# A gated two-layer transformer kernel on one core: the attention's output projection is moved from the end of a batch's loop into the first steps of the next batch's loop

## The chip, the cores and the metric

The kernel runs on one core of a Trainium2 chip. The metric is the device time of one execution in microseconds. Engine names in the profile are PE (TensorE), DVE (VectorE), ACT (ScalarE), POOL (GpSimd) and SP (SyncE, which issues the DMAs).

## What is computed

Two gated layers over x of 8 batches x 256 tokens x 512 features: attention, a ternary-weight feed-forward network, linear attention, and a mixture of experts. The change touches the first attention alone:

```
q = layernorm(x) @ Wq.T + bq                  # 32 heads of 16
k, v = ctx @ Wk.T + bk, ctx @ Wv.T + bv       # 8 groups of 16, four heads share a group
w = softmax(q k^T / 4, masked)                # 256 x 256 for each head
out = (w v) @ Wo.T + bo                       # 512 -> 512
x = x + tanh(g_xattn[0]) * out
```

Matrices are split into a high and a low 16-bit part, and a product is taken as three matmuls (high by high, high by low, low by high).

## The kernel before

The program has four phases, one after the other; the change is in phase_a (line 298), the first attention. All engines run hand-written programs in order, and semaphores (`ev[...]`) tie them together; nothing is scheduled by a planner, so the order in the code is the order on each engine.

Each batch b of eight is a body of 32 steps (NS) on ACT, POOL and DVE, and of 35 on PE. Step n of batch b is: PE writes a tile of turned scores (`turned_scores`, lines 610 and 612) into one of two PSUM banks; ACT takes the exponential of it twice, as a 16-bit and as a 32-bit tile (lines 809, 810); POOL subtracts the one from the other to get the low part (line 894); PE multiplies both with V (`times_v`, lines 628 and 630), three steps later. Every four steps DVE normalises one group of heads (`normalise`, lines 1004 to 1008) into the tile `on`.

Between these steps stands the preparation of the following batch, nx = b + 1. PE projects queries (`q_of`, 12 matmuls, lines 137 to 139) in steps 1 and 5 and keys and values (`kv_of`) in steps 3 and 7; DVE adds the biases (`bias_q`, line 956, in steps 1 and 5; `bias_kv`, lines 961 to 964, in steps 3 and 7, behind `low_q`, line 969; `low_kv`, lines 976 and 979, in steps 5 and 9). PE turns queries and keys (lines 574 and 583) in steps 9, 11, 12 and 14; the second half of the first turn waits for `dk1`, the event of line 964. From step 15 on PE computes the unturned scores of nx (`scores`, lines 595 and 598) and DVE their maxima (line 992), from which a second turn of the queries follows (`second`, line 574 again): its last part comes after step 34, and ACT copies it (`take_second`, line 756). POOL also takes apart the inputs of batch b + 2; its layer-norm moments are DVE's, line 922, at step 0.

The last thing in a body is the output projection. PE's `output(b)` (line 635) waits until the last group is normalised, makes eight transposes of `on` (line 639) into the banks BS and BS + 1, which `scores` uses later, and for each of two token tiles 12 matmuls with Wo (line 647, recorded as 137 to 139). Between them ACT takes the high part (line 830) and DVE the low part (line 1092); then DVE adds the bias and the gated residual (lines 1096 and 1099). At the start of the next body PE waits for the copies of the second turn:

```
def body(b, par, more):
    nx = b + 1
    wait("c2", b, 4, 4)
```

At the end of batch 3's body DVE also sums 32 partial sums (line 1104), for which PE waits at the start of batch 4 (line 701). Batches 4 to 7 have on ACT and DVE the cutting of the feed-forward weights to signs (lines 782 and 939). The last batch prepares no next one.

Of the kernel before, what the change touches and what calls it, by code (L numbers as in the profile page):

```python
# [19 lines left out]
ALU = mybir.AluOpType  # L20
ACT = mybir.ActivationFunctionType
# [3 lines left out]
B, S, D = 8, 256, 512  # L25
# [272 lines left out]
def phase_a(nc, a, env):  # L298
# [93 lines left out]
    TQ, TK = (9, 12), (11, 14)  # L392
    FIRST = 15
    NORM = LAG + 4

    NPIECE = 32
    ROUND = 12582912.0
# [29 lines left out]
    def bodies(body):  # L427
        for b in range(B):
            body(b, b % 2, b < B - 1)
# [13 lines left out]
    with nc.Block() as block:  # L443
# [89 lines left out]
        def _(pe):  # L533
            pe.sem_inc(ev["AV"], 4)

            def wait(n, b, count=1, per=1):
                pe.wait_ge(ev[n], b * per + count)
# [94 lines left out]
                                                skip_group_check=True)  # L632
                last.then_inc(ev["AV"], 1)

            def output(b):
                wait("ch", b, 2 * G0, 2 * G0)
                for tt in range(2):
                    for k in range(KC):
                        last = nc.tensor.transpose(bank[BS + tt][:, k * P:(k + 1) * P], on[:, tt, k * P:(k + 1) * P],
                                                   ident[:, :])  # L640
                    last.then_inc(ev[f"To{tt}"], 1)
                if b == 0:
                    pe.wait_ge(o_tp, 16 * 2 * KC)
                for tt in range(2):
                    wait(f"lO{tt}", b)
                    for k in range(KC):
                        last = env["three"](bank[BS + tt][:, :], oTh[:, tt, k, :], oTl[:, tt, k, :],
                                            woh[:, k, :], wol[:, k, :], k == 0, k == KC - 1)
                    last.then_inc(ev[f"O{tt}"], 1)


            for t in range(2):
# [41 lines left out]
# [3 lines that stand above are left out]
                wait("lv0", b)  # L697
                wait("lv1", b)
                if b == 4:
                    pe.wait_ge(t_part, 1)  # L700
                    nc.tensor.matmul(bank[BM + 1][:, 0:2], ones[:, :], sums[:, :], start=True,
                                     stop=True).then_inc(t_tot, 1)
                for n in range(NS + LAG):
                    if n < NS:
                        turned_scores(b, par, n)
                    if n >= LAG:
                        times_v(b, par, n - LAG)
                    if not more:
                        continue
                    for tt in range(2):  # L710
                        if n == PQ[tt]:
                            q_of(nx, tt)
                        if n == PK[tt]:
                            if b == 4 and tt == 0:
                                pe.wait_ge(t_red, 1)
                            kv_of(nx, tt)
                        if n == TQ[tt]:
                            wait(f"lq{tt}", nx)
                            turn_q(nx, tt, "tq")
                        if n == TK[tt]:  # L720
                            turn_k(nx, tt)

                    for m in due(n - 1):
                        scores(nx, 1 - par, m)
                    if n == HALF:
                        second(nx, 0)
                if more:
                    second(nx, 1)
                output(b)
            bodies(body)  # L730

        @block.scalar
        def _(act):
# [19 lines left out]
            def take_second(b, par, tt):  # L753
                for h in range(2):
                    wait("t2", b, 2 * tt + h + 1, 4)
                    nc.scalar.activation(qT[:, par, 8 * h:8 * h + 8, tt * P:(tt + 1) * P],
                                         bank16(BM + h).rearrange("p (j q) -> p j q", j=8), ACT.Copy)\
                      .then_inc(ev["c2"], 1)

            def normal(f, t):  # L760

# [41 lines left out]

            def body(b, par, more):
                for n in range(NS):
                    wait("ST", b, n + 1, NS)
                    wait("AV", b, n + 1, NS)
                    wait("L", b, n + 1, NS)
                    nc.scalar.activation(ph[:, n % NP, :], bank[BST + n % 2][:, :], ACT.Exp)  # L809
                    nc.scalar.activation(prob[:, n % 2, :], bank[BST + n % 2][:, :], ACT.Exp).then_inc(ev["E"], 1)  # L810
                    if summed(b, n) is not None:
                        absolute(summed(b, n))
                    if cut_piece(b, n) is not None:
                        sign(cut_piece(b, n))
                    if b + 2 < B and n in (11, 13):
                        normal(b + 2, (n - 11) // 2)
                    if not more:
                        continue
                    for tt in range(2):
                        if n == PQ[tt] + 2:  # L820
                            high_q(b + 1, tt)
                        if n == PK[tt] + 2:
                            high_kv(b + 1, 1 - par, tt)
                    if n == min(HALF + 1, NS - 1):
                        take_second(b + 1, 1 - par, 0)
                if more:
                    take_second(b + 1, 1 - par, 1)
                for tt in range(2):
                    wait(f"To{tt}", b)
                    nc.scalar.activation(oTh[:, tt], bank[BS + tt][:, :].rearrange("p (k c) -> p k c", k=KC), ACT.Copy)\  # L830
                      .then_inc(ev[f"hO{tt}"], 1)
            bodies(body)

        @block.gpsimd
        def _(pool):
# [69 lines left out]
        def _(dve):  # L905
# [105 lines left out]
                    .broadcast_to([P, 2, 4, HD0]), ALU.mult))  # L1011


            klink = Chain(dve, k_ch)
            nc.vector.memset(qs[:, :, :, :], 0.0)
            nc.vector.memset(ks[:, :, :, :, :], 0.0)
# [41 lines left out]
            def body(b, par, more):  # L1058
                link = Chain(dve, ev["ch"], b * PER)
                nx = b + 1  # L1060
                if b == 4:
                    scales()
                for n in range(NS):
                    if n >= NORM and (n - NORM) % 4 == 0:
                        normalise(link, b, (n - NORM) // 4)
                    if b + 2 < B and n == 0:
                        moments(b + 2)
                    if b + 2 < B and n == 3:
                        mean(b + 2)
                    if cut_piece(b, n) is not None:  # L1070
                        magnitude(cut_piece(b, n))
                    if not more:
                        continue
                    for tt in range(2):
                        if n == PQ[tt]:
                            bias_q(nx, tt)
                        if n == PK[tt]:
                            low_q(nx, tt)
                            bias_kv(nx, tt)
                        if n == PK[tt] + 2:  # L1080
                            low_kv(nx, 1 - par, tt)
                    for tt in range(2):
                        if n == TQ[tt]:
                            take(nx, 1 - par, tt, "q")
                        if n == TK[tt]:
                            take(nx, 1 - par, tt, "k")
                    for m in due(n):
                        maxima(nx, m)
                normalise(link, b, G0 - 1)
                for tt in range(2):  # L1090
                    wait(f"hO{tt}", b)
                    nc.vector.tensor_tensor(oTl[:, tt], bank[BS + tt][:, :].rearrange("p (k c) -> p k c", k=KC),
                                            oTh[:, tt], ALU.subtract).then_inc(ev[f"lO{tt}"], 1)
                for tt in range(2):
                    wait(f"O{tt}", b)
                    nc.vector.tensor_tensor(on[:, tt, :], bank[BS + tt][:, :], bo[:, :], ALU.add)\
                      .then_inc(ev[f"x{tt}"], 1)
                    wait(f"x{tt}", b, 3)
                    nc.vector.scalar_tensor_tensor(out=X[:, 2 * b + tt, :], in0=on[:, tt, :], scalar=tg[:, 0:1],
                                                   in1=X[:, 2 * b + tt, :], op0=ALU.mult, op1=ALU.add)  # L1100
                assert link.n == PER, link.n
                if b == 3:
                    dve.wait_ge(t_use, NPIECE)
                    nc.vector.reduce_sum(sums[:, :], part[:, :].rearrange("p (m u) -> p m u", m=2), AX_X).then_inc(t_part, 1)
            bodies(body)
    st.close()


# [1378 lines left out]
```

## Time and profile before

| | |
|---|---|
| median of 3 runs | 1948.77 us (1947.23 to 1953.24) |
| the profiled execution's own time | 1954.19 us |
| its span | 1952.4 us |
| granted TensorE clock, mean over the span | 0.95 |
| PE busy | 1677.2 us (86%) |
| VectorE busy | 1077.9 us (55%) |
| ScalarE busy | 736.4 us (38%) |
| GpSimd busy | 828.0 us (42%) |
| first exponential of batches 0, 1, 2, 7 | 70.19, 139.84, 207.23, 569.91 us |
| last residual of batch 7 starts | 625.34 us |

A row of the timeline has the start in us, the duration in us, the engine, the line, the operation with what it writes and reads, and a count; in brackets stands the idle time of the engine just before it and what ended it. Matmuls overlap, so their spacing, not their duration, is what one costs. The clock is given as a share of 2.4 GHz.

### The profile page before, as it was taken

How to read it: one execution, taken by the hardware profiler on the slowest of the kernel's cores; microseconds unless marked ns; L12 is line 12 of the kernel's file. 1: busy time of each engine (PE TensorE's matmuls, PEld its weight loads, DVE VectorE, ACT ScalarE, POOL GpSimd, SP SyncE). 2: the span in 40 equal slices, each digit the busy share in tenths (PEclk: the TensorE clock that was granted, in tenths of full speed). 3: DMA queues.
4: the chain of work that ended last, by engine and by line, in shares of the span. 5: the costliest groups of instructions: out<-in, count | busy, mean ns of one | idle time of the engine just before them, and what ended most of it. 6: DMA issues, size and time to landing. Idle time of an engine off the chain costs nothing. (4 is left out here: it accounts for less than half of the span.)

```text
span 1952.4 us, 28974 instructions
## 1 busy us (share of the span) xinstructions
PE 1677.2 (86%) x10458; PEld 864.4 (44%) x10458; DVE 1077.9 (55%) x2244; ACT 736.4 (38%) x1326; POOL 828.0 (42%) x853
## 2 busy tenths in 40 slices
PE   5798888887875588888699996999999999888897
PEld 3455545444442243443266563444444444333343
DVE  6678777768663677776155664237755333211126
ACT  2468667666665454444122321221111111122221
POOL 1668656656455344444234532523534342011134
PEclk8999999999987799999799998999999999999999
DMA  5622123123022344443335442734654554366645
GB/s 144 157 66 80 47 55 82 44 55 77 17 68 63 59 97 101 93 93 77 60 69 130 97 87 56 161 88 104 146 112 105 114 124 98 71 151 155 153 132 181
DMA packets 423499, 188.82 MB, mean 97 GB/s; under 512 B 364792, under 2 KB 387576, under 8 KB 423360
## 3 DMA queue, kind: packets, MB, share of 16 engines
q1 hardware_dynamic: 417680, 168.36, 37.9%
q0 software_dynamic: 5680, 18.62, 3.4%
q8 instruction: 86, 1.41, 0.3%
q14 instruction: 53, 0.43, 0.1%
HBM read 77.82 MB, written 22.81 MB: 52 GB/s over the span
## 5 line engine op out<-in xcount | busy, mean ns | idle before, releaser
L894 POOL TENSOR_TENSOR a_pl<-a_prob,a_ph 128x512 f16<-128x512 f32 x256 | 298.5, 1180 | 206.1 <-ACT a_prob L810 204.7
L137 PE MATMUL bank<-XTh,d_whs 128*128 128x512 f16 x512 | 194.7, 380 | 0.9 <-ACT e_y L2256 0.7
L139 PE MATMUL bank<-XTh,d_wls 128*128 128x512 f16 x512 | 194.5, 380 | 0.0
L138 PE MATMUL bank<-XTl,d_whs 128*128 128x512 f16 x512 | 194.5, 380 | 0.0
L809 ACT ACTIVATE a_ph<-bank 128x512 f16<-128x512 f32 x256 | 154.3, 603 | 100.7 <-PE bank L612 77.0
L992 DVE TENSOR_REDUCE a_mx<-bank 128x2 f32<-128x512 f32 x256 | 165.7, 684 | 32.9 <-PE bank L598 29.7
L2094 POOL CAST d_cut<-d_raw 128x512 f16<-128x512 f32 x90 | 58.0, 645 | 234.3 <-DMA d_raw<-in_L_ffn_sw 152.7
L810 ACT ACTIVATE a_prob<-bank 128x512 f32<-128x512 f32 x256 | 155.2, 606 | 0.0
L2014 DVE TENSOR_TENSOR d_hid<-d_hid,bank 128x512 f32<-128x512 f32 x64 | 43.9, 686 | 181.6 <-PE bank L139 179.7
L610 PE MATMUL bank<-a_maddT,ident 128*128 128x512 f16 x256 | 103.4, 404 | 30.1 <-ACT a_prob L810 28.2
L1227 PE MATMUL bank<-b_wfc,b_xTh 128*128 128x512 f16 x256 | 99.5, 389 | 32.3 <-DMA b_xTl<-f_cut 25.9
L1237 PE MATMUL bank<-b_wpj,b_hTh 128*128 128x512 f16 x256 | 104.6, 409 | 22.3 <-DMA b_hTl<-b_hcut 22.3
L2005 ACT ACTIVATE d_hid<-bank 128x512 f32<-128x512 f32 x64 | 38.2, 597 | 213.9 <-PE bank L139 213.9
L2106 POOL DMA_INDIRECT e_x<-rows,d_who x39 | 37.2, 953 | 191.5 <-DMA e_xTl<-e_x 185.2
L595 PE MATMUL bank<-a_madd,ident 128*128 128x512 f16 x256 | 100.0, 391 | 20.5 <-DVE a_mx L992 18.1
L2009 ACT ACTIVATE d_hh<-d_hid 128x512 f16<-128x512 f32 x64 | 40.3, 630 | 191.7 <-DVE d_hid L2014 189.0
L2096 POOL TENSOR_TENSOR d_cut<-d_raw,d_cut 128x512 f16<-128x512 f32 x90 | 105.9, 1177 | 7.2
L2024 DVE SCALAR_TENSOR_TENSOR X<-bank,tg,X 128x512 f32<-128x512 f32 x112 | 76.3, 744 | 50.5 <-PE bank L139 50.5
L1238 PE MATMUL bank<-b_wpj,b_hTl 128*128 128x512 f16 x256 | 103.8, 405 | 0.0
L612 PE MATMUL bank<-a_qT,a_kT 128*128 128x512 f16 x256 | 103.6, 405 | 0.0
L598 PE MATMUL bank<-a_kT,a_qT 128*128 128x256 f16 x512 | 99.7, 277 | 0.0
L1228 PE MATMUL bank<-b_wfc,b_xTl 128*128 128x512 f16 x256 | 99.1, 387 | 0.0
(325 smaller groups left out, 4081.5 us busy)
## 6 DMA issues: line engine op xcount, KB each, us to landing
d_raw<-in_L_ffn_w SPq DMA_DIRECT2D x48, 256.0 KB, 3.0
d_raw<-in_L_ffn_sw SPq DMA_DIRECT2D x42, 256.0 KB, 3.1
made<-e_y SPq DMA_DIRECT2D x39, 256.0 KB
a_stage<-in_L_ffn_w_fc SPq DMA_DIRECT2D x32, 256.0 KB, 2.8
a_stage<-in_L_ffn_w_proj SPq DMA_DIRECT2D x32, 256.0 KB, 3.1
a_fbuf<-in_ctx SPq DMA_DIRECT2D x16, 256.0 KB, 3.7
rows<-f_cut SPq DMA_DIRECT2D x16, 256.0 KB, 2.4
out_x<-X SPq DMA_DIRECT2D x16, 256.0 KB
```

The lines of the kernel that those rows point to most:

```text
L137: nc.tensor.matmul(out_ap, lhi, rhi, start=first, stop=False)
L138: nc.tensor.matmul(out_ap, lhi, rlo, start=False, stop=False)
L139: return nc.tensor.matmul(out_ap, llo, rhi, start=False, stop=last_one)
L610: nc.tensor.matmul(bk[:, :].rearrange("p (r k) -> p r k", r=2), ident16[:, :], maddT[:, kc, :].unsqueeze(1).broadcast_to([P, 2, S]), start ...
L612: nc.tensor.matmul(bk[:, :], kT[:, par, 2 * g + half, kc * P:(kc + 1) * P], qT[:, par, 2 * g:2 * g + 2, :].rearrange("p r q -> p (r q)"), ...
L809: nc.scalar.activation(ph[:, n % NP, :], bank[BST + n % 2][:, :], ACT.Exp)
L810: nc.scalar.activation(prob[:, n % 2, :], bank[BST + n % 2][:, :], ACT.Exp).then_inc(ev["E"], 1)
L894: nc.gpsimd.tensor_tensor(pl[:, n % NP, :], prob[:, n % 2, :], ph[:, n % NP, :], ALU.subtract).then_inc(ev["L"], 1)
L992: nc.vector.tensor_reduce(mx[:, tt, 4 * g + half:4 * g + half + 3:2], bank[BS + m % 2][:, :].rearrange("p (r k) -> p r k", r=2), AX_X, ALU ...
L1237: nc.tensor.matmul(bank[ACC + n % 2][:, :], hTh[:, n % 2, c, :], wpj[:, c, :], start=(c == 0), stop=False)
L1238: last = nc.tensor.matmul(bank[ACC + n % 2][:, :], hTl[:, n % 2, c, :], wpj[:, c, :], start=False, stop=(c == HC - 1))
L2096: nc.gpsimd.tensor_tensor(cut[:, i % RING, 1, :], raw[:, i % RING, :], cut[:, i % RING, 0, :], ALU.subtract).then_inc(p_lo, 1)
```

## The change

The output projection of batch b - 1 is issued inside batch b's loop. PE makes the transposes at step 1 (OTURN), ahead of the query projection of that step, and the 12 matmuls of each token tile at steps 4 and 5 (OUT), in step 5 again ahead of the query projection. ACT takes the high parts at the start of step 2, DVE the low parts at the start of step 2, and the bias and residual at the start of step 6. The last batch's output follows after the loop, as before.

```diff
+    OTURN, OUT = 1, (4, 5)
...
-            def output(b):
+            def turn_output(b):
                 wait("ch", b, 2 * G0, 2 * G0)
                 for tt in range(2):
                     for k in range(KC):
                         last = nc.tensor.transpose(bank[BS + tt][:, k * P:(k + 1) * P], on[:, tt, k * P:(k + 1) * P],
                                                    ident[:, :])
                     last.then_inc(ev[f"To{tt}"], 1)
-                if b == 0:
+
+            def output(b, tt):
+                if b == 0 and tt == 0:
                     pe.wait_ge(o_tp, 16 * 2 * KC)
-                for tt in range(2):
-                    wait(f"lO{tt}", b)
...
+                wait(f"lO{tt}", b)
+                for k in range(KC):
+                    last = env["three"](bank[BS + tt][:, :], oTh[:, tt, k, :], oTl[:, tt, k, :],
+                                        woh[:, k, :], wol[:, k, :], k == 0, k == KC - 1)
+                last.then_inc(ev[f"O{tt}"], 1)
...
                     if n >= LAG:
                         times_v(b, par, n - LAG)
+                    if b and n == OTURN:
+                        turn_output(b - 1)
+                    if b and n in OUT:
+                        output(b - 1, OUT.index(n))
...
-                output(b)
             bodies(body)
+            turn_output(B - 1)
+            for tt in range(2):
+                output(B - 1, tt)
...
                 for n in range(NS):
+                    if b and n == OTURN + 1:
+                        high_output(b - 1)
                     wait("ST", b, n + 1, NS)
...
                 for n in range(NS):
+                    if b and n == OTURN + 1:
+                        low_output(b - 1)
+                    if b and n == OUT[1] + 1:
+                        residual(b - 1)
                     if n >= NORM and (n - NORM) % 4 == 0:
                         normalise(link, b, (n - NORM) // 4)
...
             bodies(body)
+            low_output(B - 1)
+            residual(B - 1)
```

`high_output`, `low_output` and `residual` hold the instructions that stood at the end of the bodies of ACT and DVE, unchanged (lines 828 to 831 and 1090 to 1100); `high_output(B - 1)` follows ACT's loop.

## Rows read from the trace of the kernel before

**Rows 1.** The page, part 1: busy time, share of the span, instructions of each engine.
```profile
PE 1677.2 (86%) x10458; PEld 864.4 (44%) x10458; DVE 1077.9 (55%) x2244; ACT 736.4 (38%) x1326; POOL 828.0 (42%) x853
```
**Rows 2.** Windows: length, busy time of each engine (instructions), granted clock, DMA share, GB/s.
```profile
core 0: us, PE busy (x) PEld busy (x) DVE busy (x) ACT busy (x) POOL busy (x), PEclk, DMA share, GB/s
207.00:217.00 10.00, 10.00 (x82) 5.58 (x81) 7.24 (x15) 7.52 (x16) 7.96 (x8) 1.00 0.00 1
...
570.00:611.00 41.00, 28.96 (x300) 14.79 (x299) 21.51 (x44) 39.87 (x77) 36.05 (x31) 0.79 0.53 116
```
**Rows 3.** Timeline of ACT, seam from batch 1 to 2.
```profile
193.22 0.60 ACT L809 ACTIVATE a_ph<-bank 128x512 f16<-128x512 f32 x1
...
198.13 1.94 ACT L756 ACTIVATE a_qT<-bank 128x1024 f16<-128x1024 f16 x2 [3.82 <-PE bank L574]
199.95 1.09 ACT L830 ACTIVATE a_oTh<-bank 128x512 f16<-128x512 f32 x2
207.23 0.60 ACT L809 ACTIVATE a_ph<-bank 128x512 f16<-128x512 f32 x1 [6.18 <-PE bank L612]
```
**Rows 4.** Timeline of PE, the same seam up to batch 2's step 6.
```profile
197.47 1.07 PE L574 MATMUL bank<-ident,a_qs 128*128 128x128 f16 x16 [1.38 <-DVE a_qs L997]
198.38 1.05 PE L639 MATMUL bank<-ident,a_on 128*128 128x128 f32 x8
201.41 0.39 PE L137 MATMUL bank<-a_woh,a_oTh 128*128 128x512 f16 x1 [1.98 <-DVE a_oTl L1092]
...
206.60 0.38 PE L610 MATMUL bank<-a_maddT,ident 128*128 128x512 f16 x1
...
216.28 0.38 PE L610 MATMUL bank<-a_maddT,ident 128*128 128x512 f16 x1
```
**Rows 5.** Timeline of PE, batch 2's step 9, the second half of the first turn.
```profile
223.14 0.62 PE L574 MATMUL bank<-ident,a_qs 128*128 128x128 f16 x8 [1.75 <-DVE a_k L964]
```
**Rows 6.** Timeline of VectorE, steps 5 to 7 of batch 2.
```profile
218.68 1.28 DVE L979 TENSOR_TENSOR a_v<-a_v 128x128 f16<-128x128 f32 x1
219.93 0.70 DVE L956 SCALAR_TENSOR_TENSOR a_q<-bank,a_bq 128x512 f32<-128x512 f32 x1
...
220.56 0.19 DVE L1004 RECIPROCAL a_rec<-bank 128x8 f32<-128x8 f32 x1
...
222.80 0.28 DVE L964 TENSOR_TENSOR a_k<-bank,a_bkv 128x128 f32<-128x128 f32 x1
```
**Rows 7.** Timeline of VectorE, residual of batch 1's second token tile.
```profile
206.80 0.69 DVE L1096 TENSOR_TENSOR a_on<-bank,a_bo 128x512 f32<-128x512 f32 x1 [1.11 <-PE bank L139]
207.53 0.75 DVE L1099 SCALAR_TENSOR_TENSOR X<-a_on,tg,X 128x512 f32<-128x512 f32 x1
```
**Rows 8.** Timeline of PE and VectorE, first score matmul and later steps, batches 1 and 6.
```profile
139.21 0.38 PE L610 MATMUL bank<-a_maddT,ident 128*128 128x512 f16 x1
...
152.16 0.19 DVE L1004 RECIPROCAL a_rec<-bank 128x8 f32<-128x8 f32 x1
...
156.03 0.27 DVE L964 TENSOR_TENSOR a_k<-bank,a_bkv 128x128 f32<-128x128 f32 x1
...
497.98 0.38 PE L610 MATMUL bank<-a_maddT,ident 128*128 128x512 f16 x1
...
512.53 0.28 DVE L964 TENSOR_TENSOR a_k<-bank,a_bkv 128x128 f32<-128x128 f32 x1
```
**Rows 9.** Instructions of lines 1008 and 1099: ns min/median/max, first and last start.
```profile
L1008 DVE TENSOR_TENSOR a_on<-a_ob,a_rec x64: 291/452/1283, 84.6 to 614.5; 128x128 f32<-128x128 f32 x64
...
L1099 DVE SCALAR_TENSOR_TENSOR X<-a_on,tg,X x16: 750/752/752, 137.6 to 625.3; 128x512 f32<-128x512 f32 x16
```
**Rows 10.** Timeline of PE, seam from batch 3 to 4.
```profile
346.44 0.35 PE L701 MATMUL bank<-a_sums,a_ones 128*128 128x2 f32 x2 [1.76 <-DVE a_sums L1104]
```
**Rows 11.** PE in seams 0 to 1 and 4 to 5; window of seam 5 to 6.
```profile
131.28 1.88 PE L639 MATMUL bank<-ident,a_on 128*128 128x128 f32 x8
...
416.87 0.63 PE L138 MATMUL bank<-a_wol,a_oTh 128*128 128x512 f16 x1
417.30 0.63 PE L139 MATMUL bank<-a_woh,a_oTl 128*128 128x512 f16 x1
...
489.00:498.00 9.00, 7.76 (x28) 3.11 (x28) 2.73 (x4) 1.51 (x3) 0.00 (x0) 0.68 0.00 0
```

## What the change will do: the prediction

> **What bounds the kernel now.** I read the page first [rows 1]: PE is busy for 86% of the span, but that is a mean over stages, and only the first stage, eight batches of attention up to about 626 us, is touched. So I read windows of it [rows 2]. Directly behind the seam between batches 1 and 2, PE is busy for 10.00 of 10.00 us; and in batch 7, which prepares no next batch, ACT is busy for 39.87 of 41 us. The seam itself is seen best from ACT [rows 3]: the last exponential of batch 1 starts at 193.22, then come the copies of the second turn and the two high copies of the output projection, and then ACT idles 6.18 us until the first exponential of batch 2 at 207.23. PE's side [rows 4] shows what fills this: second turn at 197.47, the eight transposes of the output at 198.38, 1.98 us of waiting for VectorE's low part, 24 matmuls from 201.41 to 206.60, and only then the scores of batch 2. There are seven such seams.
>
> The question is what stands next. From the first score matmul of batch 2 (206.60) to that of its step 6 (216.28) [rows 4] PE has no gap: 9.68 us of scores, products with V and the projections of batch 3. Those are the steps into which the output is moved. After them VectorE sets the pace: PE's second group of turned queries waits for VectorE's key bias (line 964) [rows 5], and in program order that stands behind the bias of the second query tile, normalisation 0 and the low query [rows 6].
>
> **The change, part by part.** All times are relative to a batch's first score matmul as it is now ("zero", 206.60 for batch 2), in the seam 1 to 2.
>
> 1. The start. PE need wait only for the copies of the second turn: 198.13 + 1.94 = 200.07 [rows 3]. The batch starts at -6.5 us. That is the gross gain. PE now idles there, from the end of the second turn (198.38, rows 4) for 1.7 us, which the transposes used to fill.
>
> 2. What PE has to issue before step 6: the old 9.68, plus the transposes, 0.93 (their row has 1.05, which holds the tail of the last one; rows 4), plus 24 matmuls, 206.60 - 201.41 = 5.19 [rows 4]. Step 6 is reached at -6.5 + 9.68 + 0.93 + 5.19 = +9.3 instead of +9.7. Of 6.5 us PE keeps 0.4: what goes is the 1.98 us wait, what comes is the 1.7 us wait. No new wait of PE stands in these steps: the high copies (1.09 us on ACT, rows 3) come after step 1, while ACT would wait for step 2's scores behind the query projection anyway; behind them in ACT's queue stands only that exponential. The low parts (VectorE, step 2) stand behind the first query bias and are done about 4 us before PE's step 4.
>
> 3. VectorE. At the seam its four residual operations cover nobody's work; now they stand at step 6, between the second query bias and normalisation 0. One token tile costs 206.80 to 208.28, 1.47 us [rows 7], both 2.9 us. The output matmuls precede the query projection in PE's order, so VectorE doesn't wait for them. Query projection complete at +9.55, bias 0.63 (219.93 to 220.56, rows 6), residual 2.9: normalisation 0 starts at +13.1. Now it starts at 220.56 - 206.60 = +13.96 in batches 2 and 3, and at 152.16 - 139.21 = +12.95 in batches 1, 4 and 5 [rows 6, 8], because VectorE came late from its low key. So the residual takes idle time that the earlier start made.
>
> 4. Contention. Line 1008, with both inputs in SBUF, takes 291 ns at least and 1283 at most [rows 9], the first in the seam, where POOL is idle, the second in the steps. Line 1099 also has both inputs in SBUF and takes 750 to 752 in all 16 cases [rows 9], but all of those stand in a seam. In the steps I bound its extra between 0 and 1.0 us each, the spread of line 1008, and take the middle, 0.5 each: POOL is busy for 7.96 of 10 us in those steps [rows 2], but line 1008 isn't held each time either. Normalisation 0 comes at +14.1. By the Trainium skill, page "SBUF — State Buffer", section "Who interferes with whom", a VectorE instruction with two SBUF inputs and a GpSimd one that reads SBUF exclude each other for a whole instruction; line 1008's spread agrees. By the 750 ns row alone the six batches would be 6 us cheaper than by my sum, by the rule with every instruction blocked 6 us dearer.
>
> 5. From normalisation 0 to the end of the key bias it is 222.80 + 0.28 - 220.56 = 2.5 us in batch 2 and 156.03 + 0.27 - 152.16 = 4.1 in batch 1 [rows 6, 8]. I take 3.3. The key bias ends at +17.4, against +17.1 in batches 1, 4 and 5 and +16.5 in 2 and 3. Everything later in the batch follows it. So +0.3, +0.9, +0.9 us for batches 1 to 3. Batch 6 has no more front work, its key bias ends at 512.53 + 0.28 - 497.98 = +14.8 [rows 8]; the new one is +17.4, less the 1.9 of part 7, hence +0.7.
>
> 6. Seam 3 to 4 holds 1.76 us of PE waiting for a sum that stands behind the residual on VectorE [rows 10]. With the residual moved, the sum is ready while PE waits for the second turn's copies, so 1.8 us go: batch 4 is at +0.3 - 1.8 = -1.5.
>
> 7. Clock. Seam 4 to 5 shows output matmuls at 0.43 us spacing instead of 0.22 (0.63 against 0.38 in duration) [rows 11]; eight of them cost 1.7 us, nine in seam 5 to 6 1.9. The granted clock there was 0.68 of full speed over the seam [rows 11], 1.2 GHz in part of it. If these windows were gone, batch 5 would be at +0.3 - 1.7 = -1.4, batch 6 as given. But PE idles 1.4 us before the second turn [rows 4] and now 1.7 after it, so low-clock windows should come again, in front of a stretch in which every lost PE time counts. I take three of seven at 1.7: +5.1. The bounds are none and seven.
>
> 8. Batch 7. ACT starts 6.5 earlier, does the 1.1 us of copies, and is stopped twice, by PE's 2.6 us (half of 5.19) ahead of steps 5 and 6 each, against an ACT step of 1.3 us on average (41 / 32): about 1.5 each. -6.5 + 1.1 + 3.0 = -2.4. Its own output stays exposed at the end. No queue of SP is passed, since the step issues no DMA, and POOL has none of its work.
>
> Sum: 0.3 + 0.9 + 0.9 - 1.5 - 1.4 + 0.7 - 2.4 = -2.5 us, with the clock **+2.6 us**. The profiled execution took 1954.19 us, of it 1952.4 span; it would take 1956.8. Against the median of the three runs, 1948.77, which is 5.4 lower, the forecast is **1951.4 us**. 0.3% is 5.8 us, about what a measurement of this kernel tells from no change.
>
> **Rivals.**
> *The seam is gone* (3%): 7 x 6.5 = 45 us less, 1903. For it speaks ACT's idle time; against it PE's gapless 9.7 us. PE would need free time in steps 0 to 6, and has none.
> *A part of it stays* (14%): VectorE's operations aren't held (-6), the way to the key bias stays at 2.5 us (-5), and the clock stays up (-5): from there 6 to 13 us less, 1936 to 1943. For it speaks that PE went through seam 1 to 2 at full spacing [rows 4].
> *The residual becomes the wait* (20%). Place: VectorE, step 6. Price: both line-1099 operations held for 1.0 each and 4.1 us to the key bias, 1.8 us over my sum in each of six batches, 11 in all: 1962. It decides from 0.5 us a batch over my sum. For it speaks batch 1 with its 4.1 us; against it batch 2 with 2.5 [rows 6, 8].
> *The clock falls at every seam* (13%): four more windows of 1.7, +7: 1958. The transposes of seam 0 to 1 took 1.88 us for eight against 1.05 [rows 4, 11], so idle time of this size can bring it. The Trainium skill, page "TensorE: Matmul & The Clock Gate", section "HAM oscillation — how this bites in real kernels", says that waits between bursts of matmuls make the clock fall again and again; by that this rival would be the likeliest. The full spacing of seam 1 to 2 is against it [rows 4].
> That the change doesn't do what it says is out: each engine issues in program order.
>
> **How the numbers follow.** Forecast 50%, by itself 1946 to 1954.5. The others as above. Faster by over 0.3%: 3 + 14 = 17%. Slower: 20 + 13 = 33%. Within: 50%. The range reaches down into the partial gain and up to the residual's price: 1941 to 1963.
>
> **What would show it.** Right: in seam 1 to 2 some 7.5 us from the last to the first exponential instead of 14.0; then 15.8 us without a gap on PE up to step 6; ACT idle 3 to 4 us ahead of step 6; PE waiting for line 964 at +17.4. Wrong: gaps on PE in steps 0 to 5, line 1099 at 1.2 us or more with everything behind it late, low-clock matmuls in most seams, or steps 10 to 31 of a batch of another length than now.

## The result, and the profile after

| | before | after |
|---|---|---|
| median | 1951.45 us (20 runs, 1945.20 to 1958.97) | 1957.01 us (20 runs, 1953.27 to 1963.53) |
| ratio | | 1.0025, 95% interval 1.0015 to 1.0035 |
| span of the profiled execution | 1952.4 us | 1951.6 us |
| its first attention stage, first exponential to last residual's start | 70.19 to 625.34 = 555.15 us | 68.61 to 627.73 = 559.12 us |

The change costs a quarter of a per cent: 0.0025 x 1951.45 is 4.9 us more. The forecast was 2.6 more. The spans of the two profiled executions differ the other way, but by less than executions of one kernel differ; the stage alone is 4.0 us longer.

The page of the changed kernel, part 1 (busy time, share, instructions), is to be read beside [rows 1]; the counts are the same:

```profile
PE 1684.2 (86%) x10458; PEld 872.2 (45%) x10458; DVE 1074.7 (55%) x2244; ACT 737.9 (38%) x1326; POOL 831.9 (43%) x853
```

The timeline of ACT in the seam between batches 1 and 2, to be read beside [rows 3]:

```profile
193.56 0.60 ACT L825 ACTIVATE a_ph<-bank 128x512 f16<-128x512 f32 x1
...
198.46 1.94 ACT L764 ACTIVATE a_qT<-bank 128x1024 f16<-128x1024 f16 x2 [3.82 <-PE bank L575]
201.53 0.60 ACT L825 ACTIVATE a_ph<-bank 128x512 f16<-128x512 f32 x1 [1.12 <-PE bank L613]
...
203.45 1.12 ACT L771 ACTIVATE a_oTh<-bank 128x512 f16<-128x512 f32 x2
206.91 0.60 ACT L825 ACTIVATE a_ph<-bank 128x512 f16<-128x512 f32 x1 [2.34 <-PE bank L613]
...
218.31 0.60 ACT L825 ACTIVATE a_ph<-bank 128x512 f16<-128x512 f32 x1 [3.92 <-PE bank L613]
```

The seam has shrunk from 14.0 to 8.0 us, as intended. But ACT now waits 2.34 us for PE ahead of step 2 and 3.92 ahead of step 6. PE's timeline says why, beside [rows 4, 5]:

```profile
197.81 1.07 PE L575 MATMUL bank<-ident,a_qs 128*128 128x128 f16 x16 [1.38 <-DVE a_qs L1010]
200.46 0.61 PE L611 MATMUL bank<-a_maddT,ident 128*128 128x512 f16 x1 [1.58 <-ACT a_qT L764]
200.85 0.63 PE L613 MATMUL bank<-a_qT,a_kT 128*128 128x512 f16 x1
...
203.69 0.38 PE L137 MATMUL bank<-a_wqh,a_xTh 128*128 128x512 f16 x1
...
217.68 0.38 PE L611 MATMUL bank<-a_maddT,ident 128*128 128x512 f16 x1
...
225.25 1.03 PE L575 MATMUL bank<-ident,a_qs 128*128 128x128 f16 x8 [3.12 <-DVE a_k L977]
```

From the first score matmul (200.46) to that of step 6 (217.68) are 17.22 us with no idle time in the trace, where 9.68 stood before. The first matmuls last 0.61 and 0.63 us instead of 0.38. PE then waits 3.12 us for the key bias instead of 1.75. Two windows, the start of the stretch and the whole of it:

```profile
200.40:203.60 3.20, 3.14 (x12) 2.12 (x13) 0.02 (x1) 2.08 (x6) 0.91 (x1) 0.51 0.01 3
200.40:217.70 17.30, 17.24 (x105) 9.46 (x106) 6.47 (x12) 9.01 (x20) 9.42 (x9) 0.91 0.07 17
```

The granted clock is 0.51 of full speed up to the query projection, which is the 1.2 GHz level, and 0.91 over the whole. PE is busy for 17.24 of 17.30 us. VectorE from the second query bias to the key bias, beside [rows 6, 8]:

```profile
217.92 0.71 DVE L969 SCALAR_TENSOR_TENSOR a_q<-bank,a_bq 128x512 f32<-128x512 f32 x1 [2.62 <-issue]
...
218.56 0.67 DVE L1036 TENSOR_TENSOR a_on<-bank,a_bo 128x512 f32<-128x512 f32 x1
219.26 0.75 DVE L1039 SCALAR_TENSOR_TENSOR X<-a_on,tg,X 128x512 f32<-128x512 f32 x1
219.93 0.69 DVE L1036 TENSOR_TENSOR a_on<-bank,a_bo 128x512 f32<-128x512 f32 x1
220.65 0.93 DVE L1039 SCALAR_TENSOR_TENSOR X<-a_on,tg,X 128x512 f32<-128x512 f32 x1
221.51 0.20 DVE L1017 RECIPROCAL a_rec<-bank 128x8 f32<-128x8 f32 x1
...
222.78 0.98 DVE L982 TENSOR_TENSOR a_qs<-a_q,a_qs 128x512 f16<-128x512 f32 x1
...
224.92 0.28 DVE L977 TENSOR_TENSOR a_k<-bank,a_bkv 128x128 f32<-128x128 f32 x1
```

VectorE idles 2.62 us, adds the query bias, and then does the residual (218.56 to 221.51) ahead of normalisation 0, the low query and the key bias, for which PE waits.

Where the 4.0 us of the stage lie, from the two timelines. From the last exponential of the batch before to the end of the key bias, batches 1 to 6: +0.8, +1.8, +2.9, 0.0, +0.2, +2.8, together +8.5. From there to the batch's last exponential: -0.2, -1.9, -2.0, -1.1, -0.3, 0.0, together -5.4. Batch 7 with its seam: -0.6. The rest is in batch 0, whose code is unchanged (+1.3, so not the change's), and behind the last batch (+0.2). Batch 4's 0.0 has in it that the 1.76 us wait of [rows 10] is gone.

### The profile page after: what moved, and what is told of

It reads as the page before. It is cut to its first block and busy times, and to the rows that moved or that the text cites. A ratio compares the mean times of both kernels' runs of the same rounds, so it can differ in the third digit from the quotient of the medians.

```text
span 1951.6 us, 28973 instructions
## 1 busy us (share of the span) xinstructions
PE 1684.2 (86%) x10458; PEld 872.2 (45%) x10458; DVE 1074.7 (55%) x2244; ACT 737.9 (38%) x1326; POOL 831.9 (43%) x853
## 5 line engine op out<-in xcount | busy, mean ns | idle before, releaser
L907 POOL TENSOR_TENSOR a_pl<-a_prob,a_ph 128x512 f16<-128x512 f32 x256 | 304.6, 1203 | 201.3 <-ACT a_prob L826 199.7
L611 PE MATMUL bank<-a_maddT,ident 128*128 128x512 f16 x256 | 107.4, 420 | 37.6 <-ACT a_prob L826 28.0
L1260 PE MATMUL bank<-b_wpj,b_hTh 128*128 128x512 f16 x256 | 107.1, 418 | 23.7 <-DMA b_hTl<-b_hcut 23.7
L596 PE MATMUL bank<-a_madd,ident 128*128 128x512 f16 x256 | 98.8, 386 | 20.7 <-DVE a_mx L1005 18.4
```

Of the source, the lines that this page charges most:

```text
L611: nc.tensor.matmul(bk[:, :].rearrange("p (r k) -> p r k", r=2), ident16[:, :], maddT[:, kc, :].unsqueeze(1).broadcast_to([P, 2, S]), start ...
L907: nc.gpsimd.tensor_tensor(pl[:, n % NP, :], prob[:, n % 2, :], ph[:, n % NP, :], ALU.subtract).then_inc(ev["L"], 1)
L1260: nc.tensor.matmul(bank[ACC + n % 2][:, :], hTh[:, n % 2, c, :], wpj[:, c, :], start=(c == 0), stop=False)
```

## The experiments

The theories. **P**: PE's row of work up to step 6 has no gap, so what the seam gives is paid back there. **V**: the residual at VectorE's step 6 stands ahead of the key bias. **C**: the low clock behind each seam costs on the path. The rival to P is that the moved matmuls are covered and something else eats the seam. In each diff the kernel that it starts from is named.

### One product instead of three, in both kernels

In the changed kernel:

```diff
-                    last = env["three"](bank[BS + tt][:, :], oTh[:, tt, k, :], oTl[:, tt, k, :],
-                                        woh[:, k, :], wol[:, k, :], k == 0, k == KC - 1)
+                    last = nc.tensor.matmul(bank[BS + tt][:, :], oTh[:, tt, k, :], woh[:, k, :],
+                                            start=k == 0, stop=k == KC - 1)
```

> The changed kernel with one product (high by high) instead of three in the output projection: 8 matmuls in a batch instead of 24, 3.5 us of PE time less. The low parts of the output and of Wo are left out of the result. Theory P: step 6 comes 3.5 us earlier; VectorE then waits for its own low key part, so 2.6 us a batch in batches 1 to 6, some 2 in batch 7 and 3.5 at the exposed end: about 21 us less than the changed kernel, ratio to the kernel before 0.992. If PE's work in these steps is covered by others: 3.5 us less, ratio 1.001.

Measured: 0.993 (0.991 to 0.995), that is 18 to 19 us below the changed kernel. The same cut in the kernel before:

> The kernel before with one product instead of three in the output projection (the low parts of the output and of Wo are left out of the result). All of the 24 matmuls stand in a seam there, 3.5 us of them gone in each of eight: 28 us less, ratio 0.986. Under theory P the same cut is worth nearly as much in the changed kernel (19 us were measured from 1.0025 to 0.993), which it could not be if the moved matmuls were covered.

Measured: 0.9867 (0.9837 to 0.9897), 26 us below. There eight cuts of 3.5 us stand bare in the seam and give 26 of 28. In the changed kernel, where seven of them stand beside the loop's work, the runs still gave 18 to 19. Part of that is not the matmuls: in this profile two of the seven seams, those into batches 2 and 4, passed at full clock, and in the changed kernel's none did, which in these two batches is worth 1.5 and 2.2 us (by the two profiles of the next section). Batch 2 shows the rest at full clock: PE's row up to step 6 takes 12.29 us, and 15.75 in the kernel with all three products at full clock (below), so the cut takes 3.5 us out of it. The moved work is not covered, and P holds. But from step 6 to the end of the key bias it now takes 9.79 us instead of 7.51, so of the 3.5 us only about 1.2 reach the key bias. VectorE's timeline in the changed kernel with one product, batch 2:

```profile
212.98 0.28 DVE L992 TENSOR_TENSOR a_v<-a_v 128x128 f16<-128x128 f32 x1
213.22 0.70 DVE L969 SCALAR_TENSOR_TENSOR a_q<-bank,a_bq 128x512 f32<-128x512 f32 x1
```

The second query bias now follows the low parts of key and value without a gap: with less work on PE, VectorE's own chain is the bound, as it was in the kernel before [rows 6].

### Unread matmuls in PE's waits

In the changed kernel, with FILL = (6, 7):

```diff
+            def fill(count):
+                for i in range(count):
+                    nc.tensor.matmul(bank[BST][:, :], woh[:, 0, 0:P], woh[:, 1, :], start=True, stop=True)
...
                 if more:
+                    fill(FILL[0])
                     second(nx, 1)
+                    fill(FILL[1])
```

> The changed kernel with matmuls whose result nobody reads in PE's two waits of the seam: six ahead of the second turn's last part, seven behind it. Theory C (low clock behind the seam costs about 1.5 us in each of seven batches): the first score matmuls of a batch are at 0.22 us spacing again and the eight output transposes at 1.05 us, 7 to 10 us less than the changed kernel, ratio to the kernel before 0.997 to 0.999. If the clock costs nothing on the path: 1.0025, or a little more where the added matmuls are late.

Measured: 0.9972 (0.9959 to 0.9985), 5.3 us below the kernel before and 10.3 below the changed one. PE's timeline of the same seam:

```profile
195.35 1.67 PE L699 MATMUL bank<-a_woh 128*128 128x512 f16 x7
197.09 0.39 PE L612 MATMUL bank<-a_maddT,ident 128*128 128x512 f16 x1
...
198.84 0.38 PE L137 MATMUL bank<-a_wqh,a_xTh 128*128 128x512 f16 x1
```

From the first score matmul to the query projection it takes 1.75 us instead of 203.69 - 200.46 = 3.23: 1.5 us of low clock in this seam. In the changed kernel the first four matmuls of a batch are long (0.59 to 0.63 us) behind all seven seams, in this one (0.38 or 0.39) behind none. PE's row up to step 6 is 15.73 to 15.75 us in batches 1 to 6, and 17.2 to 18.3 in the changed kernel. With the seams, the way from the last exponential to the key bias is shorter by 1.5 to 2.6 us a batch, 12.3 in these six, by the two profiles; batch 7 with its seam is 0.9 longer. C holds, with a price that I had taken for three seams. The Trainium skill, page "TensorE: Matmul & The Clock Gate", section "HAM oscillation — how this bites in real kernels", says that waits between bursts of matmuls bring the clock down each time; its case has longer waits, for DMAs. In the changed kernel the trace agrees, seven of seven, with waits of 1.4 and 1.2 to 1.6 us. Not every such seam is slow: with the same two waits (1.39 and 1.58 us) the kernel with one product went through the seam into batch 2 at full clock.

The kernel before, filled in its own waits (six ahead of the second turn, eight between the output's transposes and matmuls):

```diff
+    FILL = (6, 8)
...
                     last.then_inc(ev[f"To{tt}"], 1)
+                if b < B - 1:
+                    fill(FILL[1])
...
                 if more:
+                    fill(FILL[0])
                     second(nx, 1)
```

> The kernel before with unread matmuls in its own waits of the seam: six ahead of the second turn's last part, eight between the output's transposes and its matmuls. Its low-clock windows in the seams (17 matmuls in two seams, transposes in two more) should go: 4 to 5 us less, ratio 0.9975. Theory P then says that at the same clock the change is worth nothing or little: this run and the changed kernel with the same filling (0.9972) agree within 0.2%. If the seam's 6.5 us had been gained and lost to the clock alone, this one would stay well above the filled changed kernel.

Measured: 0.9989 (0.9972 to 1.0005). All its seams but that into batch 4 are at 14.0 us then, so the two low windows of seams 4 to 5 and 5 to 6 are gone. Between the two filled kernels lie 0.17% or 3.3 us in favour of the change, with overlapping intervals. At the same clock the change is worth about 3 us or nothing, and not 45: P again.

### The residual elsewhere on VectorE

The first of these runs puts it behind the key bias, through a tile of its own, since normalisation 0 overwrites `on` in step 7:

```diff
+    ro = sb("a_ro", [P, 2, D])
...
-                    if b and n == OUT[1] + 1:
+                    if b and n == 8:
                         residual(b - 1)
```

> The changed kernel with the bias and residual of the output at VectorE's step 8 (behind the key bias of step 7) instead of step 6, through a tile of their own. Theory P (PE's gapless row of work from the first score matmul to step 6 pays the seam back): step 6 on PE comes as in the changed kernel. Theory V (the residual on VectorE delays the key bias): normalisation 0 comes 2.9 us earlier, the low query then waits for ACT's high query, which ends 1.3 us before the low query starts now, so the key bias ends 1.3 us earlier in six batches: 6 to 8 us less than the changed kernel, ratio to the kernel before 0.998 to 1.000. If only P holds, the ratio stays at 1.0025.

Measured: 1.009 (1.007 to 1.011): 13 us worse than the changed kernel instead of 6 to 8 better. VectorE's and PE's timelines, batch 2:

```profile
228.16 0.67 DVE L1037 TENSOR_TENSOR a_ro<-bank,a_bo 128x512 f32<-128x512 f32 x1
228.87 1.73 DVE L1040 SCALAR_TENSOR_TENSOR X<-a_ro,tg,X 128x512 f32<-128x512 f32 x1
...
232.09 1.37 DVE L990 TENSOR_TENSOR a_ks<-a_k,a_ks 128x256 f16<-128x256 f32 x1
```
```profile
235.36 0.91 PE L585 MATMUL bank<-ident,a_ks 128*128 128x128 f16 x7 [5.20 <-DVE a_qT L1000]
```

The key bias did come about 1.4 us earlier after the batch's first exponential (22.3 instead of 23.7), as V had it; from PE's step 6 to its end it takes 5.51 us instead of 7.51. But the residual now holds the low key and the copies behind it for 232.09 - 228.16 = 3.9 us, and PE waits 5.20 us for them. V's first half holds, and the assumption that nothing behind the key bias is tight falls.

The second run puts it in step 5, where VectorE idles: the first token tile ahead of the low key, the second between it and the second query bias.

```diff
-            def residual(b):
-                for tt in range(2):
+            def residual(b, tt):
...
-                    if b and n == OUT[1] + 1:
-                        residual(b - 1)
+                    if b and n == OUT[1]:
+                        residual(b - 1, 0)
...
+                        if b and n == OUT[1] and tt:
+                            residual(b - 1, 1)
                         if n == PQ[tt]:
                             bias_q(nx, tt)
```

> The changed kernel with the residual at VectorE's step 5: the first token tile ahead of the low key, the second behind it and ahead of the second query bias, where VectorE waits for ACT and PE (1.5 and 2.6 us in batch 2). Theory V: the low query then waits for ACT's high query instead of the residual, the key bias ends 1.3 us earlier in six batches and nothing behind it is held: 8 us less than the changed kernel, ratio to the kernel before 0.998 to 0.999. Theory P alone (PE sets the key bias): 1.0025, unchanged.

Measured: 0.9993 (0.9977 to 1.0009), 6.2 us below the changed kernel and level with the kernel before. V holds, but the total is near its price of 8 by two errors that offset each other. From PE's step 6 to the end of the key bias it takes 5.50 us instead of 7.51 in batches 1 to 5, and 13.0 us less in six, where I had 8. And "nothing behind it is held" was wrong: from the key bias to the last exponential the six batches are 6.9 us longer than in the changed kernel. VectorE's low part of the values, an operation with both inputs in SBUF, takes 1.23 or 1.24 us instead of 0.28 in five of them, because a subtraction of GpSimd is running when it starts. Residual early and waits filled, both together:

> The residual at step 5 as in the run before and the unread matmuls in PE's two waits of the seam. Theories V and C together, which act on different waits: 8 and 10 us add up, ratio to the kernel before 0.993 (0.991 to 0.995). If they share one path they don't add: 0.997 as with the matmuls alone.

Measured: 0.9918 (0.9894 to 0.9941), median 1936.51 us: the fastest of the kernels here that compute everything. That is 20.9 us below the changed kernel, where the two parts alone had given 6.2 + 10.3 = 16.5; the interval holds that sum too. They act on different waits and add up: PE's row up to step 6 is at 15.73 to 15.75 us, as with the matmuls alone, and from there to the key bias it is 5.50 us, as with the early residual alone. VectorE's timeline of batch 2, and below it GpSimd's row beside the last line:

```profile
212.38 0.68 DVE L1042 TENSOR_TENSOR a_on<-bank,a_bo 128x512 f32<-128x512 f32 x1
213.09 0.75 DVE L1045 SCALAR_TENSOR_TENSOR X<-a_on,tg,X 128x512 f32<-128x512 f32 x1
214.00 1.14 DVE L996 TENSOR_TENSOR a_ks<-a_k,a_ks 128x256 f16<-128x256 f32 x1 [0.16 <-ACT a_ks L766]
...
215.27 0.68 DVE L1042 TENSOR_TENSOR a_on<-bank,a_bo 128x512 f32<-128x512 f32 x1
215.98 0.75 DVE L1045 SCALAR_TENSOR_TENSOR X<-a_on,tg,X 128x512 f32<-128x512 f32 x1
217.50 0.71 DVE L976 SCALAR_TENSOR_TENSOR a_q<-bank,a_bq 128x512 f32<-128x512 f32 x1 [0.77 <-issue]
...
221.09 0.79 DVE L989 TENSOR_TENSOR a_qs<-a_q,a_qs 128x512 f16<-128x512 f32 x1 [1.96 <-ACT a_qs L758]
...
224.78 1.24 DVE L999 TENSOR_TENSOR a_v<-a_v 128x128 f16<-128x128 f32 x1
```
```profile
224.54 1.34 POOL L877 TENSOR_TENSOR a_fcut<-a_fbuf,a_fcut 128x512 f16<-128x512 f32 x1
```

The residual stands in what was idle, and the second query bias is no later for it. What is left ahead of the key bias is 1.96 us of waiting for ACT's high query, and behind it the held low value (224.78). Against the kernel before with its own waits filled (0.9989) the moved output is now worth 0.71% or 14 us, with intervals that stand apart.

### Two more places

The output matmuls in PE's wait for the key bias, with the residual through a tile `ro` as above:

```diff
-    OTURN, OUT = 1, (4, 5)
+    OTURN, OUT = 1, (8, 9)
```

> The changed kernel with the 24 output matmuls in steps 8 and 9 instead of 4 and 5, and the residual at step 10, through a tile of its own; the transposes stay in step 1. Theory P: steps 4 and 5 lose 5.2 us of PE work, step 6 comes 5 us earlier and the key bias 3 to 4; the matmuls fall into PE's wait for the key bias (3.1 us in batch 2), the rest of 2 us and 2.9 us of VectorE come behind it: 1 to 3 us less per batch, ratio to the kernel before 0.990 to 0.998. Theory V alone, or a bound elsewhere: the ratio stays within 0.2% of 1.0025.

Measured: 1.0008 (0.9992 to 1.0024), 3.3 us below the changed kernel with intervals that overlap: less than P had it, and not clearly a gain. The key bias of batch 2 ends 18.4 us after the first exponential instead of 23.7, more than expected; but the residual, then at step 10, stands ahead of the key copies:

```profile
225.78 0.68 DVE L1037 TENSOR_TENSOR a_ro<-bank,a_bo 128x512 f32<-128x512 f32 x1
226.49 1.39 DVE L1040 SCALAR_TENSOR_TENSOR X<-a_ro,tg,X 128x512 f32<-128x512 f32 x1
...
228.52 0.92 DVE L1040 SCALAR_TENSOR_TENSOR X<-a_ro,tg,X 128x512 f32<-128x512 f32 x1
...
230.63 1.29 DVE L1000 COPY a_kT<-bank 128x1024 f16<-128x1024 f16 x2
```

and the exponential of step 14 comes 32.4 us after the first one, where it came after 32.7 in the changed kernel. The gain is taken back within four steps.

Last, the remaining wait of the fastest kernel:

```diff
-                        if n == PQ[tt] + 2:
+                        if n == PQ[tt] + 2 - tt:
                             high_q(b + 1, tt)
```

> The kernel with the residual at step 5 and the filled waits, and ACT's high part of the second query tile at step 6 instead of 7. With the residual out of the way VectorE idles 1.96 us ahead of the second low query and waits for that high part, which stands behind exponential 7. If that wait is the one left ahead of the key bias, the key bias ends about 1 us earlier in batches 1 to 6: 6 us less, ratio to the kernel before 0.989. If another wait takes over within that microsecond (VectorE's low key and copies behind it): unchanged, 0.992.

Measured: 0.996 (0.9947 to 0.9974), so neither: 8 us worse than the fastest kernel, with intervals that stand apart. The key bias came 1.5 us earlier, but the next instruction of that chain, the second low key, now idles longer:

```profile
224.02 1.03 DVE L996 TENSOR_TENSOR a_ks<-a_k,a_ks 128x256 f16<-128x256 f32 x1 [2.98 <-ACT a_ks L766]
```

ACT's high key has its place behind exponential 9, which two more operations in front of exponential 7 delay; exponential 10 starts 22.0 us after the first one instead of 21.8. So the query copies behind the low key start 24.2 us after the first exponential instead of 23.8: the earlier key bias is a loss of 0.4 us there. In its profile the stage is 6.3 us longer than that of the fastest kernel (548.6 against 542.3). Batches 1 to 6 are 8.4 us shorter up to the key bias and 12.9 longer behind it, of which the later copies are the part that is shown; the rest of it stays open. Batch 7, whose code is the same, has another 1.6 (48.2 against 46.6); it also took 48.2 in the changed kernel with the filled waits.

## Why the prediction was right, point by point

The forecast was +2.6 us, its likeliest case a change of less than 0.3%, and +4.9 (0.25%) was measured. On the forecast's base of 1948.77 us that is 1953.6, inside the likeliest case (1946 to 1954.5) and the range; the median of 1957.01 stands beside a later median of 1951.45 for the kernel before. The mechanism was the predicted one: PE has no gap up to step 6 and pays the seam back there. That the number came so close is luck: the clock cost 5 to 7 us more than taken, the residual's hold 5 us less, and the way behind the key bias gave 5.4 us that I had at nothing.

- *Start and PE* (parts 1 and 2): the seam of 7.5 us came out at 8.0; PE has no gap up to step 6, but takes 17.2 us instead of 15.8. The 1.4 too much are the clock of this seam: with filled waits it took 15.73 to 15.75 in all six batches. The low parts were ready 0.9 us before PE's first output matmul (208.42 against 209.28), not 4.
- *The residual's hold by POOL* (part 4): I took 1.0 us a batch, the changed kernel shows 0.18 (0.75 and 0.93), so 5 us too much in six batches. At its place POOL had idled for 4.66 us and began its next subtraction at 219.47, when the first of the two was already running. Two steps later in the code the same operation took 1.73. The size hangs on what POOL does at that time, which I read from the old window; and line 1008, from which I took the spread, has its 0.29 us not only in the seam but also in eleven steps. By the Trainium skill, page "SBUF — State Buffer", section "Who interferes with whom", a VectorE instruction with two SBUF inputs and a GpSimd one that reads SBUF contend; these durations agree.
- *From normalisation 0 to the key bias* (part 5): 3.7 us in batches 1 to 5 and 4.2 in batch 6, 3.3 taken.
- *"Everything later in the batch follows it"* (part 5) is the step that failed. From the key bias on, batches 2 to 4 were 1.1 to 2.0 us shorter than before, 5.4 in all six, and all of it before the exponential of step 14. In batches 2 and 3, 1.2 us each lie ahead of VectorE's query copies: there GpSimd held the low part of the values before, and no longer does. In batch 2, before (two rows) and after:

```profile
225.34 1.24 DVE L979 TENSOR_TENSOR a_v<-a_v 128x128 f16<-128x128 f32 x1
225.09 1.33 POOL L857 TENSOR_TENSOR a_fcut<-a_fbuf,a_fcut 128x512 f16<-128x512 f32 x1
```
```profile
227.21 0.28 DVE L992 TENSOR_TENSOR a_v<-a_v 128x128 f16<-128x128 f32 x1
```

  In batch 4 the copies start at the same distance from the key bias in both kernels (2.2 us), and of the 1.1 us some 0.8 are one turn of the queries that fell into the low clock before (1.87 us) and not after (1.05). The rest was not taken apart. The work behind the key bias doesn't simply follow it: what it meets there is shifted too.
- *The sum of batch 3* (part 6): seen; batch 4 is level with before despite its low clock.
- *Clock* (part 7): the term was mis-sized. Seven of seven seams fell, at 1.5 us in the seam into batch 2 and up to 2.6, 10.3 us in all by the runs, against 5.1. The rival "the clock falls at every seam" came true as an event; its time (1958) did not, because of the residual's hold and the way behind the key bias.
- *Batch 7* (part 8): ACT was stopped by 1.36 and 1.53 us, as predicted (1.5 each). A third wait was missed: the weights' scaling on VectorE stands behind the residual, and ACT waits 1.73 us for it. -0.6 instead of -2.4:

```profile
575.16 0.60 ACT L825 ACTIVATE a_ph<-bank 128x512 f16<-128x512 f32 x1 [1.36 <-PE bank L613]
...
578.38 0.60 ACT L825 ACTIVATE a_ph<-bank 128x512 f16<-128x512 f32 x1 [1.53 <-PE bank L613]
...
582.17 0.72 ACT L796 ACTIVATE a_tern<-a_stage,a_unround 128x512 f16<-128x512 f32 x1 [1.73 <-DVE a_stage L952]
```

- *The residual becomes the wait* (rival): not with the price given, but it was there; moving it to idle time gave 6.2 us at the low clock.

## What to carry to other kernels

Work that is moved off a bare seam gains only where its engine has free time at the new place; here 6 us a seam became 3 us in all, at equal clock, since PE had no gap for the next 9.7 us. With the residual in VectorE's idle time it became 14. Move each engine's share on its own: the same residual cost 13 us more two steps later and 6 less one step earlier, in a wait that the change itself had made. A shorter seam can still hold the waits that lower TensorE's clock, and if dense PE work follows, filling them pays.

## What was not expected

Thirteen matmuls that nobody reads, 13 x 0.22 = 2.8 us of TensorE work in each of seven seams, took 10.3 us off the kernel. In the kernel before, filled in the same way, 2 us with an interval that reaches no change. The same instruction (the gated residual, 128 x 512) took 0.75, 0.93, 1.39 or 1.73 us in the rows above; it took 0.75 where GpSimd was idle or left a gap between two instructions just after its start (213.15 to 213.24 in the fastest kernel), and longer where GpSimd's subtractions ran on without one.
